# Ternary weights inside the first causal attention, and wider query loads in grouped attention

## The chip, the core and the metric

The kernel is one program on one core of a Trainium2 chip. The metric is the device time of that program in microseconds (us), the median of several runs. The core has a matrix engine (TensorE, PE in the profile, with its weight loads as PEld), VectorE (DVE), ScalarE (ACT), GpSimd (POOL) and a queue engine that starts DMAs (SyncE, SP). Each has its own instruction stream; they meet through semaphores.

## What is computed

Eight layers act in turn on a residual stream X of 2 x 1024 tokens by 256 features. The layers that the change touches are the first three and the fifth:

```python
# 1: causal attention, 16 heads of 128
q, k, v = x @ w_q + b_q, x @ w_k + b_k, x @ w_v + b_v
out = softmax(mask(q k^T / sqrt(128))) v @ w_o + b_o
# 2 and 4: feed-forward layer with ternary weights (2048x256 and 256x1024), groups of 64
w = w_fp32.astype(bfloat16)
scale = clip(mean(abs(w_g)), 1e-8)          # w_g: groups of 64
q = clip(round(w_g / scale), -1, 1)
wq = w + stop_gradient(q * scale - w)
h = silu(x @ wq_gate.T) * (x @ wq_up.T);  y = rms_norm(h) @ wq_proj.T
# 5: grouped-query attention, 32 query heads of 8, 8 key heads, rotary positions, no mask
```

Layer 3 is a delta rule, layers 6 and 8 feed-forward layers with Hadamard-transformed weights, and layer 7 a causal attention with ALiBi. The input of each layer is normalised.

## The kernel before

`program` (line 1784) calls the layers one after another. Each opens a block that all engines enter and leave together. X stays in SBUF for the whole program.

**First attention** (`causal_attention`, line 156, called as "at1"). The work is 32 "halves" n (batch times 16 heads), each of 8 query tiles u, so 256 units U = 8n + u. The order of work is written out by hand: `others(U)` and `turns(U)` list the items that follow the scores of unit U (projections q, k, v; transposed probabilities t; attention times values pv; output projection o; and c, which adds a bias product in every second half). Every item uses one of four PSUM banks in turn, and TensorE waits before item i until VectorE has finished with item i - 4. ScalarE takes the high part of each result (`high`, L521), VectorE the low part (`low`, L616). SyncE loads the weights of a pair of heads (`load`) when GpSimd has split the last pair.

**Ternary stage** (`ternary_weights`, line 667, called as "tq1" and "tq2"). It loads the weights by one DMA for each call and works through 8 and 4 slices of 128 x 512: ScalarE casts a slice to bf16 (L703) and takes its magnitude (L707), TensorE averages it over groups by one matmul (L718), VectorE clips the mean, makes two comparisons and four further steps (L735 to L750), and ScalarE copies the result into the float32r weights (L697).

**Feed-forward layer** (`ffn`, line 753, "ff2" and "ff4"). It begins with statistics on VectorE (L938), an inverse root on GpSimd (L905), the scaled X on VectorE (L950), transposes on TensorE (L835), high part on ScalarE (L886), low part on VectorE (L955), and then the gate and up products (L792), which read the ternary weights.

**Grouped attention** (`grouped_attention`, line 1260). A first block writes the queries and keys, split in three bf16 parts, to DRAM (`qs`, `ks`; L1323). The main block (L1326 on, "ga5m") has 16 units n (batch times key head) in 3 buffer slots, each in two halves of the queries, so 32 halves h. GpSimd issues the loads of a unit in `load` (L1390 for keys, L1395 for queries: 6 + 24 DMAs), three units at the start and then unit n + 2 after the first half of unit n, once TensorE has finished the scores of unit n - 1. For each half, TensorE makes 16 rows of scores (L1455), VectorE takes their maxima (L1538) and copies them, transposed, to mT (L1543); GpSimd splits the maxima in three bf16 parts (`split`, L1404 to L1414), and SyncE copies them into rows 48 to 50 of the query tile by 12 small DMAs (L1435). Only then do the key scores of that half run (L1479), followed by exponentials on ScalarE (L1521) and products with the values (L1492). On GpSimd `split(h + 1)` stands behind the loads that were issued after `split(h)`. On TensorE the first 11 rows of half 1 stand ahead of the first key scores.

Of the kernel before, what the change touches and what calls it, by code (L numbers as in the profile page):

```python
# [155 lines left out]
def causal_attention(nc, name, X, consts, pack, cap_dram, slopes=None, out_bias=None):  # L156
# [9 lines left out]
    with Scope(nc, name) as s:  # L166
# [24 lines left out]
        if out_bias is not None:  # L191
            bsum = s.sb("bsum", [P, D])
            bvT = [s.sb(f"bvT{p}", [P, 2, P], F32R) for p in "hl"]
        S = [s.ps(f"S{i}", [P, SEQ]) for i in range(2)]
# [12 lines left out]
        def others(U):  # L207
# [37 lines left out]
        for x in order:  # L245
            if x[0] not in ("c", "o"):
                high_no[x] = len(high_no) + 1
# [32 lines left out]
        def _(sp):  # L280
# [6 lines left out]

            def load_slope(n):
# [101 lines left out]
        def _(pe):  # L390
# [30 lines left out]
            def use(x):  # L421
# [19 lines left out]
                elif kind == "v":  # L441
# [44 lines left out]
        def _(act):  # L486
# [55 lines left out]

            act.wait_ge(prep_done, 4)
            for what in ("qk0", "v", "qk1", "o") + (("bv",) if out_bias is not None else ()):
                split(0, what)
            for U in range(0, LAST + 1):
                for x in others(U - 1):
                    if x[0] == "o":
                        scaled_out(x)
                    elif x[0] != "c":  # L550
# [6 lines left out]
                m = n // 2 + 1  # L557
                if m < NPAIR:
# [12 lines left out]
        def _(dve):  # L571
# [13 lines left out]
            def low(x):  # L585
                kind, n, i = x
                src = bank(x)[:, :]
                if kind == "c":
# [4 lines left out]
                    return  # L593
                dve.wait_ge(high_done, high_no[x])
# [21 lines left out]
                nc.vector.tensor_tensor(lo, src, hi.bitcast(F32), ALU.subtract).then_inc(low_done, 1)  # L616

# [28 lines left out]
            for U in range(0, LAST + 1):  # L646
# [20 lines left out]
def ternary_weights(nc, name, consts, w_dram, dst, chunks, width):  # L667


    with Scope(nc, name) as s:  # L670
        NCOL = 512
        n = chunks * width // NCOL
        raw = s.sb("raw", [P, chunks * width])
        wb = s.sb("wb", [P, chunks * width], BF16)
        mag = s.sb("mag", [P, 2, NCOL], BF16)
        sc = s.sb("sc", [P, 2, NCOL], BF16)
        up = s.sb("up", [P, NCOL], BF16)
        dn = s.sb("dn", [P, NCOL], BF16)
        sign = s.sb("sign", [P, NCOL], BF16)
        q = s.sb("q", [P, NCOL], BF16)  # L680
        dlt = s.sb("dlt", [P, NCOL], BF16)
        out = [s.sb(f"out{i}", [P, NCOL], BF16) for i in range(2)]
        mean = [s.ps(f"mean{i}", [P, NCOL]) for i in range(2)]
        raw_in, cast_done, mag_done, mean_done, step = (s.sem(x) for x in ("raw", "cast", "mag", "mean", "step"))
        sc_done, out_done, put_done = s.sem("sc"), s.sem("out"), s.sem("put")
        block = s.block()
        dflat = dst.rearrange("p c n -> p (c n)")

        @block.sync
        def _(sp):  # L690
            sp.dma_start(raw[:, :], w_dram).then_inc(raw_in, 16)

        @block.scalar
        def _(act):
            def put(i):
                act.wait_ge(out_done, i + 1)
                nc.scalar.activation(dflat[:, i * NCOL:(i + 1) * NCOL], out[i % 2][:, :],  # L697
                                     ACT.Copy).then_inc(put_done, 1)

            act.wait_ge(raw_in, 16)  # L700
            for i in range(n):
                c = slice(i * NCOL, (i + 1) * NCOL)
                nc.scalar.activation(wb[:, c], raw[:, c], ACT.Copy).then_inc(cast_done, 1)  # L703
# [1256 lines left out]
```

## Time and profile before

| | us |
|---|---|
| median of 3 runs | 3988.59 (3968.72 to 3989.05) |
| the profiled execution, its own time | 3988.94 |
| its span, first to last instruction | 3987.10 |
| first attention | about 10 to 967 |
| ternary stage | 967 to 1031 |
| first ternary feed-forward layer | from 1031 |
| main block of grouped attention | 1749 to 2607 |

Over the span PE is busy 88%, DVE 66%, ACT 56% and POOL 30%. A line of the profile's timeline gives the start, the duration, the engine, the line of the kernel, the tiles written and read, the shapes, how many instructions are merged in it, and in square brackets how long the engine had been idle before and what ended that idle time.

### The profile page before, as it was taken

To read this page: it belongs to the slowest core of one execution; us is meant where nothing else is said; L and a number is where in the kernel's file an instruction comes from. 1 tells how busy PE (TensorE), PEld (TensorE's weight loads), DVE (VectorE), ACT (ScalarE), POOL (GpSimd) and SP (SyncE) were. 2 spreads that over 40 slices of the span, in tenths; PEclk is the share of its full clock that TensorE was granted. 3 is DMA by queue.
4 is the path that set the end of the run, shared out by engine and by line. 5 is a ranking of instruction groups with operands and counts; after the bars stand their busy time and mean duration, and the time that the engine had idled before them with its cause. 6 is when DMAs were issued, how large, how long until landed. Compare 5 with 4: busy or idle time off the path is not lost. (4 is left out here: it accounts for less than half of the span.)

```text
span 3987.1 us, 66189 instructions
## 1 busy us (share of the span) xinstructions
PE 3517.8 (88%) x24420; PEld 2673.4 (67%) x24420; DVE 2631.2 (66%) x4953; ACT 2248.1 (56%) x4552; POOL 1184.8 (30%) x1598
## 2 busy tenths in 40 slices
PE   7999999996578988738888889969799999999979
PEld 6999999996457977512222222248789888888868
DVE  5666666666655665447778777624588788878843
ACT  5777777775433324215667666723467666667732
POOL 2323243331232443253333333030232332232210
PEclk9999999998789998857889888989999999999989
DMA  1000000000000000020000000020111010110010
GB/s 61 17 16 22 22 12 22 22 12 22 11 17 5 0 1 3 18 65 17 22 22 22 22 22 22 2 112 1 43 38 41 29 38 27 42 39 27 27 64 22
DMA packets 46547, 104.76 MB, mean 26 GB/s; under 512 B 28374, under 2 KB 29142, under 8 KB 39976
## 3 DMA queue, kind: packets, MB, share of 16 engines
q1 hardware_dynamic: 18408, 84.83, 6.1%
q0 software_dynamic: 27840, 15.91, 1.7%
q8 instruction: 192, 3.15, 0.3%
q14 instruction: 107, 0.88, 0.1%
HBM read 87.87 MB, written 12.32 MB: 25 GB/s over the span
## 5 line engine op out<-in xcount | busy, mean ns | idle before, releaser
L1538 DVE TENSOR_REDUCE ga5m_nm<-ga5m_M 128x1 f32<-128x1024 f32 x512 | 602.4, 1220 | 171.2 <-PE ga5m_M L1455 161.3
L1521 ACT ACTIVATE ga5m_pr<-ga5m_E 128x512 f32<-128x512 f32 (+1 forms) x683 | 535.0, 811 | 296.3 <-PE ga5m_E L1479 284.9
L352 POOL TENSOR_TENSOR all_X<-all_X,at_part 128x512 f32<-128x512 f32 x256 | 335.4, 1310 | 992.7 <-ACT at_part L532 992.6
L1479 PE MATMUL ga5m_E<-ga5m_Q,ga5m_K 51*128 51x512 bf16 x1024 | 295.4, 419 | 85.6 <-DMA ga5m_Q<-ga5m_mpart 69.7
L417 PE MATMUL at_A<-all_ident,at_prob 128*128 128x128 f32 x2304 | 340.1, 274 | 31.4 <-ACT at_prob L540 22.1
L1492 PE MATMUL ga5m_O<-ga5m_pr,ga_Vx 128*32 128x256 f32 x4096 | 353.2, 424 | 0.0
L1455 PE MATMUL ga5m_M<-ga5m_K,ga5m_Q 48*128 48x512 bf16 x1024 | 255.0, 430 | 61.1 <-DMA ga5m_Q<-ga_qs 43.9
L417 PEld LDWEIGHTS at_A<-all_ident,at_prob 128*128 128x128 f32 x2304 | 265.0, 140 | 60.3 <-DVE at_q1l L600 26.7
L616 DVE TENSOR_TENSOR at_pT1l<-at_A,at_pT1h 128x512 fp32r<-128x512 f32 (+1 forms) x384 | 235.8, 642 | 64.6 <-ACT at_pT1h L521 58.0
L1479 PEld LDWEIGHTS ga5m_E<-ga5m_Q,ga5m_K 51*128 51x128 bf16 x1024 | 68.4, 96 | 313.0 <-issue 164.8
L631 DVE CUSTOM_DVE_ANT_0 at_prob<-at_prob,at_slope 128x128 f32<-128x128 f32 (+7 forms) x256 | 231.5, 904 | 8.8
L965 DVE TENSOR_TENSOR ff_hf<-ff_sil,ff_up 128x512 f32<-128x512 f32 x128 | 87.8, 686 | 220.0 <-ACT ff_sil L871 220.0
L871 ACT ACTIVATE ff_sil<-ff_gate 128x512 f32<-128x512 f32 x128 | 76.8, 600 | 272.1 <-PE ff_up L792 272.1
L631 DVE CUSTOM_DVE_ANT_0 at_S<-at_S,at_cap 128x128 f32<-128x128 f32 (+7 forms) x256 | 194.9, 761 | 44.4 <-PE at_S L395 44.4
L521 ACT ACTIVATE at_pT1h<-at_A 128x512 fp32r<-128x512 f32 (+1 forms) x384 | 202.0, 563 | 28.4 <-PE at_A L417 22.5
L1492 PEld LDWEIGHTS ga5m_O<-ga5m_pr,ga_Vx 128*32 128x32 f32 x4096 | 86.7, 112 | 193.1 <-issue 156.6
L1395 POOL DMA_DIRECT2D ga5m_Q<-ga_qs x384 | 213.7, 583 | 7.6 <-issue 7.6
L625 DVE SCALAR_TENSOR_TENSOR at_prob<-at_S,at_cap 128x128 f32<-128x128 f32 (+7 forms) x256 | 192.5, 752 | 23.5 <-PE at_S L395 23.5
L540 ACT ACTIVATE at_prob<-at_prob,at_nmin 128x128 f32<-128x128 f32 (+7 forms) x256 | 198.0, 773 | 7.6 <-DVE at_nmin L631 7.4
L540 ACT ACTIVATE at_prob<-at_S,at_nmin 128x128 f32<-128x128 f32 (+7 forms) x256 | 189.8, 741 | 1.7 <-DVE at_nmin L631 1.7
L616 DVE TENSOR_TENSOR at_pT0l<-at_A,at_pT0h 128x128 fp32r<-128x128 f32 (+2 forms) x384 | 167.2, 463 | 4.1 <-ACT at_pT0h L521 3.1
L521 ACT ACTIVATE at_pT0h<-at_A 128x128 fp32r<-128x128 f32 (+2 forms) x384 | 147.5, 419 | 28.4 <-PE at_A L417 28.1
(384 smaller groups left out, 10702.1 us busy)
## 6 DMA issues: line engine op xcount, KB each, us to landing
at_raw<-in_pack SPq DMA_DIRECT2D x32, 1027.0 KB, 5.2
at_slope<-in_slopes SPq DMA_DIRECT2D x32, 512.0 KB, 4.2
ga5m_Q<-ga_qs POOLq DMA_DIRECT2D x128, 48.0 KB, 2.2
ga5m_Q<-ga5m_mpart SPq DMA_DIRECT2D x384, 1.0 KB
ga5m_Q<-ga_qs POOLq DMA_DIRECT2D x128, 32.0 KB, 2.2
ga_qs<-ga5s_part SPq DMA_DIRECT2D x6, 512.0 KB
all_X<-in_x SPq DMA_DIRECT2D x1, 2048.0 KB, 7.4
tq_raw<-in_gu SPq DMA_DIRECT2D x1, 2048.0 KB, 7.8
```

What stands on the lines that cost most here:

```text
L352: nc.gpsimd.tensor_tensor(X[:, t:t + 2, :], X[:, t:t + 2, :], part[(i - 1) % 2][:, :, :], ALU.add).then_inc(added, 1)
L417: mm = nc.tensor.transpose(bank(x)[:, (kt % 4) * P:(kt % 4 + 1) * P], prob[u % 4][:, kt * P:(kt + 1) * P], consts["ident"][:, :])
L521: nc.scalar.activation(out, src, ACT.Copy).then_inc(high_done, 1)
L540: nc.scalar.activation(prob[u % 4][:, 0:end], src[:, 0:end], ACT.Exp, bias=nmin[:, at(U):at(U) + 1], scale=-1.0, accum_out=rsum[:, at(U):a ...
L616: nc.vector.tensor_tensor(lo, src, hi.bitcast(F32), ALU.subtract).then_inc(low_done, 1)
L631: nc.vector.tensor_tensor_reduce(out=src, in0=src, in1=add, scale=1.0, scalar=FAR, op0=ALU.add, op1=ALU.min, accum_out=nmin[:, at(U):at(U) ...
L1395: pool.dma_start(Q[n % SLOTS][x][rows, a, :], qs[head:head + 1, q, :, cols].broadcast_to([w, HD, SEQ])).then_inc(q_in[n % SLOTS], 16)
L1455: mm = nc.tensor.matmul(out[:, x * 512:(x + 1) * 512], Q[n % SLOTS][x][at:at + NROW, a, q0:q0 + P], K[n % SLOTS][at:at + NROW, x * 512:(x ...
L1479: mm = nc.tensor.matmul(Eb[:, e % 3, :], K[n % SLOTS][rows, kt * P:(kt + 1) * P], Q[n % SLOTS][0][rows, j // 2, qh * 512:(qh + 1) * 512], ...
L1492: mm = nc.tensor.matmul(Ob[32 * j:32 * j + 32, cols], Vx[:, b * QT + kt, kv, :], pr[:, (k * NQ + j) % NR, cols], start=(kt == 0 and half = ...
L1521: nc.scalar.activation(pr[:, a % NR:a % NR + b - a, :].rearrange("p a n -> p (a n)"), Eb[:, a % 3:a % 3 + b - a, :].rearrange("p a n -> p ...
L1538: nc.vector.tensor_reduce(nm[h % 2][:, r:r + 1], src[:, :], AX.X, ALU.max, negate=True).then_inc(m_read, 1)
```

## The change

The ternary stage goes. `causal_attention` gets an argument `ternary` and makes one slice in each of the halves 0 to 11, kept as bf16; `ffn` converts the twelve slices to float32r at its start, nine on ScalarE and three on GpSimd. In grouped attention, the queries of one unit lie in DRAM so that one DMA brings all four heads (the host permutes the weights' columns to match), each slot holds one query tile where it held two, and six DMAs carry the maxima where twelve did.

```diff
 def others(U):  # first attention
+            if ternary is not None and u == 7 and n < NTERN:
+                out.append(("w", n, 0))
 # SyncE
             for m in range(1, NPAIR):
                 load(m)
+                load_ternary(2 * m - 2)
+                load_ternary(2 * m - 1)      # each 128x512 f32, waits for the cast of the slice before
 # TensorE
+                elif kind == "w":
+                    pe.wait_ge(tmag_done, n + 1)
+                    mm = nc.tensor.matmul(out[:, :], consts["group"][:, :], tmag[:, :], start=True, stop=True)
 # ScalarE
+                if ternary is not None and u == 5 and n < NTERN:
+                    magnitude(n)             # cast to bf16, then Abs
 # VectorE
+                if kind == "w":
+                    dve.wait_ge(full, pos[x] + 1)
+                    nc.vector.tensor_scalar(tsc[:, :], src[:, :], 1e-8, None, ALU.max).then_inc(low_done, 1)
+                    return
...
+                if ternary is not None and 1 <= n <= NTERN and u < 4:
+                    ternary_step(n - 1, u)   # step 0: two comparisons; 1, 2, 3: one tensor_tensor each
+                    if u == 3:
+                        ternary_step(n - 1, 4)
 # ffn, TensorE, behind the transposes and ahead of the gate products
+            if convert is not None:
+                pe.wait_ge(act_conv, len(convert) - POOL_PART)
+                pe.wait_ge(pool_conv, POOL_PART)
 # ffn, ScalarE, ahead of x_high(0, 0)
+            if convert is not None:
+                for dst, src in convert[POOL_PART:]:
+                    nc.scalar.activation(dst, src, ACT.Copy).then_inc(act_conv, 1)
 # ffn, GpSimd, behind inverse_std(0)
+            if convert is not None:
+                for dst, src in convert[:POOL_PART]:
+                    nc.gpsimd.tensor_copy(dst, src).then_inc(pool_conv, 1)
 # grouped attention, stores
-                            dst = qs[m * 16:(m + 1) * 16, k] if i < 2 else ks[:, k]
-                            sp.dma_start(dst, part[i][0:M, k, :]).then_inc(stored, 16)
+                            if i == 2:
+                                sp.dma_start(ks[k], part[i][0:M, k, :]).then_inc(stored, 16)
+                                continue
+                            for t in range(TOK // 512):
+                                sp.dma_start(qs[k, 4 * m:4 * m + 4, :, t], part[i][:, k, t * 512:(t + 1) * 512]
+                                             ).then_inc(stored, 16)
 # grouped attention, loads
-                            for x in range(2):
-                                for a in range(HPG):
-                                    head = kv * NQ + 2 * a + (g + x) % 2
-                                    pool.dma_start(Q[n % SLOTS][x][rows, a, :],
-                                                   qs[head:head + 1, q, :, cols].broadcast_to([w, HD, SEQ])
-                                                   ).then_inc(q_in[n % SLOTS], 16)
+                            pool.dma_start(Q[n % SLOTS][rows, :, :, :],
+                                           qs[q:q + 1, kv, :, 2 * b:2 * b + 2].rearrange("o d t s n -> o d (t s n)")
+                                           .broadcast_to([w, HD, 2 * NQ * 512])).then_inc(q_in[n % SLOTS], 16)
 # grouped attention, maxima
-                            for a in range(HPG):
-                                at = 8 * g + 4 * a
-                                sp.dma_start(Q[n % SLOTS][0][row:row + 1, a, qh * 512:(qh + 1) * 512]
-                                             .rearrange("o (t n) -> o t n", n=P),
-                                             mpart[at:at + 4, x, :]).then_inc(max_in, 16)
+                            sp.dma_start(Q[n % SLOTS][row:row + 1, qh, 2 * g:2 * g + 2, :]
+                                         .rearrange("o s (t n) -> o (s t) n", n=P),
+                                         mpart[8 * g:8 * g + 8, x, :]).then_inc(max_in, 16)
 # program
-            ternary_weights(nc, "tq1", consts, io["gu0"], w1[0], DC, 2 * FF)
-            ternary_weights(nc, "tq2", consts, io["pr0"], w2[0], FC, D)
```

## Rows read from the trace of the kernel before

**Rows 1.** Windows view, busy us (count) by engine, then PE clock, DMA share, GB/s

```profile
967.18:1031.06 63.88, 7.31 (x12) 1.26 (x12) 43.32 (x85) 21.55 (x36) 0.00 (x0) 0.50 0.14 50
50.00:437.00 387.00, 387.00 (x2755) 360.17 (x2754) 248.82 (x573) 276.35 (x646) 117.25 (x110) 1.00 0.06 20
```

**Rows 2.** Timeline at the two ends of the ternary stage

```profile
967.18 0.33 SPq L691 DMA_DIRECT2D tq_raw<-in_gu  x1
...
1031.06 1.40 DVE L938 BATCH_NORM_STATS2 ff_stats<-all_X 128x6 f32<-128x256 f32 x4 [0.97 <-PEq L55]
```

**Rows 3.** Groups by line in the ternary stage: busy us, mean ns of one

```profile
L738 DVE SCALAR_TENSOR_TENSOR tq_up<-tq_sc,tq_wb 128x512 bf16<-128x512 bf16 x12 | 8.3, 693 | 0.4
...
L697 ACT ACTIVATE tern_w<-tq_out 128x512 fp32r<-128x512 bf16 x12 | 7.5, 629 | 28.8 <-DVE tq_out L750 28.8
...
L718 PE MATMUL tq_mean<-tq_mag,all_group 128*128 128x512 bf16 x12 | 7.3, 609 | 53.1 <-ACT tq_mag L707 53.1
```

**Rows 4.** Timeline of VectorE in the first attention: unit 7 of three successive halves

```profile
121.82 1.23 DVE L631 CUSTOM_DVE_ANT_0 at_S<-at_S,at_cap 128x1024 f32<-128x1024 f32 x1 [0.59 <-PE at_S L395]
...
150.48 1.23 DVE L631 CUSTOM_DVE_ANT_0 at_S<-at_S,at_cap 128x1024 f32<-128x1024 f32 x1 [0.60 <-PE at_S L395]
...
179.81 1.23 DVE L631 CUSTOM_DVE_ANT_0 at_S<-at_S,at_cap 128x1024 f32<-128x1024 f32 x1 [0.59 <-PE at_S L395]
```

**Rows 5.** Timeline at the start of half 4 of the first attention

```profile
185.05 1.16 DVE L616 TENSOR_TENSOR at_pT1l<-at_A,at_pT1h 128x512 fp32r<-128x512 f32 x2 [1.58 <-ACT at_pT1h L521]
```

**Rows 6.** Start of the feed-forward layer: timeline, and one GpSimd group

```profile
1033.28 1.04 POOL L905 TENSOR_TENSOR ff_rstd<-ff_vare,all_minus_half 128x4 f32<-128x4 f32 x1
...
1036.94 0.60 ACT L886 ACTIVATE ff_XT0h<-ff_xp 128x512 fp32r<-128x512 f32 x1 [6.19 <-PE ff_xp L835]
...
1039.17 0.79 PE L792 MATMUL ff_gate<-ff_XT0h,tern_w 128*128 128x512 f32 x1 [1.41 <-DVE ff_XT0l L955]
...
L915 POOL COPY ff_acc<-ff_sq 128x512 f32<-128x512 f32 x1 | 0.7, 698 | 13.2 <-ACT ff_sq L882 13.2
```

**Rows 7.** Timeline of the start of grouped attention's main block

```profile
1750.07 3.38 POOL L1381 DMA_DIRECT2D ga5m_K<-in_krows  x6 [38.59 <-POOLq L55]
...
1771.31 1.04 PE L1455 MATMUL ga5m_M<-ga5m_K,ga5m_Q 48*128 48x512 bf16 x4 [43.87 <-DMA ga5m_Q<-ga_qs]
...
1791.21 0.27 DVE L1543 COPY ga5m_mT<-ga5m_M 16x128 f32<-16x128 f32 x1
...
1801.20 0.61 PE L1455 MATMUL ga5m_M<-ga5m_K,ga5m_Q 48*128 48x512 bf16 x2 [0.53 <-DVE ga5m_nm L1538]
...
1802.47 7.50 SPq L1435 DMA_DIRECT2D ga5m_Q<-ga5m_mpart  x12
...
1811.04 0.61 PE L1479 MATMUL ga5m_E<-ga5m_Q,ga5m_K 51*128 51x512 bf16 x2 [9.23 <-DMA ga5m_Q<-ga5m_mpart]
```

**Rows 8.** Query-load issues on GpSimd: ns min/median/max, first and last start

```profile
L1395 POOL DMA_DIRECT2D ga5m_Q<-ga_qs x384: 521/594/644, 1754.0 to 2483.9; - x192
```

**Rows 9.** Timeline of halves 2 to 4 of grouped attention

```profile
1842.53 0.28 DVE L1543 COPY ga5m_mT<-ga5m_M 16x128 f32<-16x128 f32 x1
...
1863.38 0.28 DVE L1543 COPY ga5m_mT<-ga5m_M 16x128 f32<-16x128 f32 x1 [0.44 <-PE ga5m_M L1461]
...
1870.94 0.28 POOL L1404 CAST ga5m_mpart<-ga5m_mT 16x128 bf16<-16x128 f32 x1
...
1879.75 0.61 PE L1479 MATMUL ga5m_E<-ga5m_Q,ga5m_K 51*128 51x512 bf16 x2 [4.01 <-DMA ga5m_Q<-ga5m_mpart]
...
1893.66 0.28 DVE L1543 COPY ga5m_mT<-ga5m_M 16x128 f32<-16x128 f32 x1 [2.18 <-PE ga5m_M L1461]
```

**Rows 10.** Last copy of maxima, and windows without and behind a wait

```profile
2570.14 0.28 DVE L1543 COPY ga5m_mT<-ga5m_M 16x128 f32<-16x128 f32 x1 [1.21 <-PE ga5m_M L1461]
...
1843.00:1864.00 21.00, 20.29 (x205) 5.45 (x197) 19.64 (x20) 16.97 (x22) 10.90 (x23) 1.00 0.10 26
...
1876.00:1894.00 18.00, 14.21 (x73) 3.33 (x73) 8.37 (x10) 7.54 (x10) 0.00 (x0) 0.55 0.00 0
```

More of the change, by code:

```diff
@@ L193, in causal_attention @@
             bvT = [s.sb(f"bvT{p}", [P, 2, P], F32R) for p in "hl"]
+        if ternary is not None:
+            t_src, t_out = ternary
+            NTERN = len(t_src)
+            traw = s.sb("traw", [P, 512])
+            twb, tmag, tsc, tup = (s.sb(f"t{x}", [P, 512], BF16) for x in ("wb", "mag", "sc", "up"))
+            tdn = tmag
+            traw_in, tcast_done, tmag_done = s.sem("traw_in"), s.sem("tcast_done"), s.sem("tmag_done")
+            tstep, tern_done = s.sem("tstep"), s.sem("tern_done")
         S = [s.ps(f"S{i}", [P, SEQ]) for i in range(2)]
@@ L664, in _ @@
                         normalise(1, 2 * (u - 3) + 1)
[L667 to L703, printed above, removed]
-                act.wait_ge(cast_done, i + 1)
-                if i >= 2:
-                    act.wait_ge(mean_done, i - 1)
-                nc.scalar.activation(mag[:, i % 2, :], wb[:, c], ACT.Abs).then_inc(mag_done, 1)
-                if i >= 1:
-                    put(i - 1)
-            put(n - 1)
-        @block.tensor
-        def _(pe):
-            for i in range(n):
-                pe.wait_ge(mag_done, i + 1)
-                if i >= 2:
-                    pe.wait_ge(sc_done, i - 1)
-                nc.tensor.matmul(mean[i % 2][:, :], consts["group"][:, :], mag[:, i % 2, :],
-                                 start=True, stop=True).then_inc(mean_done, 1)
-        @block.vector
-        def _(dve):
-            k = [0]
-            def then(op):
-                k[0] += 1
-                op.then_inc(step, 1)
-                dve.wait_ge(step, k[0])
-            for i in range(n):
-                c = slice(i * NCOL, (i + 1) * NCOL)
-                dve.wait_ge(mean_done, i + 1)
-                nc.vector.tensor_scalar(sc[:, i % 2, :], mean[i % 2][:, :], 1e-8, None, ALU.max).then_inc(sc_done, 1)
-                dve.wait_ge(sc_done, i + 1)
-                nc.vector.scalar_tensor_tensor(up[:, :], sc[:, i % 2, :], 257.0 / 512.0, wb[:, c],
-                                               ALU.mult, ALU.is_lt).then_inc(step, 1)
-                nc.vector.scalar_tensor_tensor(dn[:, :], sc[:, i % 2, :], -257.0 / 512.0, wb[:, c],
-                                               ALU.mult, ALU.is_gt).then_inc(step, 1)
-                k[0] += 2
-                dve.wait_ge(step, k[0])
-                then(nc.vector.tensor_tensor(sign[:, :], up[:, :], dn[:, :], ALU.subtract))
-                then(nc.vector.tensor_tensor(q[:, :], sign[:, :], sc[:, i % 2, :], ALU.mult))
-                then(nc.vector.tensor_tensor(dlt[:, :], q[:, :], wb[:, c], ALU.subtract))
-                if i >= 2:
-                    dve.wait_ge(put_done, i - 1)
-                nc.vector.tensor_tensor(out[i % 2][:, :], wb[:, c], dlt[:, :], ALU.add).then_inc(out_done, 1)
@@ L753, in ffn @@
[L753 removed]
+def ffn(nc, name, X, consts, w1, w2, rms, weights_in=None, convert=None):
     H, L = 0, 1
@@ L1916, in rope, with rotary @@
         return np.ascontiguousarray(np.stack([np.cos(ang), np.sin(ang) * sign], axis=1).astype(f32))
-    def rotary(w, width):
+    spread = np.arange(P) // 4 % 8
+    q_order = np.arange(256).reshape(8, 2, 2, 8).transpose(0, 3, 2, 1).ravel()
+    k_order = np.arange(64).reshape(2, 4, 8).transpose(0, 2, 1).ravel()
+    def rotary(w, width, order=slice(None)):
         wt = w.T
-        swapped = wt.reshape(D, -1, 2, width // 2)[:, :, ::-1, :].reshape(D, -1)
+        swapped = wt.reshape(D, -1, 2, width // 2)[:, :, ::-1, :].reshape(D, -1)[:, order]
+        wt = wt[:, order]
         return np.ascontiguousarray(np.stack([chunks(wt), chunks(swapped)], axis=1))
```

79 lines of the change are left out of this document (58 added, 21 removed).

## The prediction

> **What bounds the kernel now.** I read four views in this order: the table of windows stage by stage, the timeline where stages meet, the groups by line inside the ternary stage, and then, in grouped attention, every copy of maxima to mT, because one copy marks one half.
>
> First attention: in 387 us TensorE is busy for all 387.0, at clock 1.00, VectorE 248.8 and ScalarE 276.4 [rows 1]. So TensorE sets the pace, and what is added to it there adds to the time one for one. VectorE has 138 us free, in 13.5 halves of 28.7 to 29.3 us [rows 4], some 10 us in each.
>
> Ternary stage: from the DMA at 967.18 to the first statistics of the next layer at 1031.06, 63.9 us [rows 2], in which TensorE works 7.3 us and VectorE 43.3 [rows 1]. Nothing else runs beside it.
>
> Grouped attention: mT(2), mT(3) and mT(4) come at 1842.53, 1863.38 and 1893.66 [rows 9]: one half took 20.85 us, the next 30.28. In the short one VectorE is busy 19.6 of 21 us at clock 1.00 [rows 10]; it paces that half. In the long one mT(3) is ready at 1863.38, but GpSimd starts to split it at 1870.94, since it was issuing the loads of a later unit, and TensorE stands idle 4.01 us for the maxima [rows 9]. Then, from 1876 to 1894, it runs only 73 matmuls in 14.2 busy us (195 ns each, against 99 ns before the wait), at a mean granted clock of 0.55, so mostly at the lower level, 1.2 GHz [rows 10]. The timeline has 13 such long halves, one for each unit loaded inside the loop.
>
> **The change part by part.** The sum is made against the profiled execution: span 3987.10, own time 3988.94, which is 0.35 above the median of 3988.59.
>
> *Ternary stage removed: -63.9* [rows 2]. One block boundary stays, as there was one at each end.
>
> *Slices inside the first attention: +7.* TensorE gets 12 matmuls of 512 columns. Halves with the bias item c last 29.33, those without 28.66 [rows 4]; c is six products of 256 columns, so 1536 columns cost 0.67 us and 512 cost 0.22, together 2.7. The upper end for one is its 0.61 in the ternary stage, at half clock [rows 3], together 7.3. VectorE gets 43.3/12 = 3.6 us a slice and ScalarE two activations of some 0.62 [rows 1, 3]; both have that much free in a half. But VectorE's share is bunched at units 0 to 3: the clip and two comparisons of 0.69 each [rows 3] stand at unit 0. The clip falls into the 1.58 us that VectorE waits for ScalarE there [rows 5]; the comparisons come behind it, and push back the low parts that TensorE needs before it may reuse a bank four items later. I put what then reaches TensorE at 0.35 us a slice, 4.2 in all; with 2.7 that is 7. Ends: nothing of it (+3 in all), or all of VectorE's and ScalarE's work, 12 x (3.6 + 1.2) = 58. I am near the low end, because both engines wait, on average, a third of the time. Below +3 it can't go, TensorE having no gap to fill. The SyncE queue gains twelve loads: each waits for the cast of the slice before (unit 5 of a half), and behind it stands the load of a pair's weights, which is released at unit 3 of a later half anyway; no delay.
>
> *Conversion to float32r in the feed-forward layer: 0.* ScalarE is idle until 1036.94, 5.9 us after the layer's start; nine copies of 0.63 [rows 3] take 5.7. GpSimd is free at 1034.3, and TensorE starts the products at 1039.17 [rows 6]: three copies may take 1.6 us each, and the nearest row has 0.70 [rows 6]. What hides them is the chain of statistics, inverse root and transposes. Were that cover gone, it would be 5.7.
>
> *Start of the grouped loop: -18.* Before: 6 + 30 issues, then the first rows at 1771.31, 21.2 us after 1750.07 [rows 7]. That is 0.55 us an issue and 1.4 for landing (one instruction is 0.52 to 0.64 [rows 8]; they overlap a little). Now: 6 + 12 issues, 9.9 + 1.4 = 11.3; I add 1.2, since each query DMA brings four times the bytes: +12.5. mT(0) follows 19.9 later, at +32.4; the 42 issues are over at +23, so the split doesn't wait. What is late next is TensorE's own order: 11 rows of half 1 stand ahead of the first key scores and end 10.6 after mT(0) (1801.81 less 1791.21 [rows 7]), at +43.0. The maxima are there sooner: 12 DMAs took 7.5 us [rows 7], six take 3.75, with 0.3 ahead and 1.1 behind 5.2, at +37.9. First key scores were at +61.0 (1811.04), so 18.0 is gained.
>
> *The 13 waits inside the loop: -123.* From mT(2) to mT(31) are 29 halves in 2570.14 - 1842.53 = 727.6 us [rows 9, 10]. Twelve issues in place of 30 free GpSimd 18 x 0.55 = 9.9 us sooner, at 1861.0, ahead of mT(3). Maxima then land at about 1863.4 + 0.3 + 5.2 = 1868.9, and TensorE wanted them at 1875.7: 6.8 us to spare. With the wait goes the low clock behind it, and VectorE's 20.85 is left: 29 x 20.85 = 604.7, a gain of 122.9. That a half keeps this pace with loads beside it is what the half from 1842.53 shows. Six query issues could each be 1.5 us longer ((6.8 + 2.4)/6) before the wait comes back.
>
> *Stores: +1.* 24 query stores in place of 6, on SyncE, between casts of ScalarE; only the last four can stick out. Bounds 0 and 18 x 0.6 = 11.
>
> Sum: 3988.9 - 63.9 + 7 + 0 - 18 - 122.9 + 1 = **3792 us**.
>
> Two rules beside it. By the Trainium skill's page "DMA: Bandwidth & Descriptors" (section "Why a DMA increments its semaphore by 16 and not by 1"), a DMA uses as many engines as divide the slowest dimension of both sides; a query load repeats three or two times there, so two or three engines would carry 64 KB each. At the page's 436 GB/s over 16 engines I estimate 2.4 us in place of 0.6 for this, and a sum of 3793. No row shows it. Of VectorE and GpSimd the result is a rival below.
>
> **The rivals.**
> (a) *Query issues cost by their bytes.* If GpSimd needs four times 0.58 for four times the bytes, a load takes 6 x 0.55 + 6 x 2.3 = 17 us as before (16.5). The start gains nothing (+18), and of the 4.01 us wait 3.75 are saved by the shorter train of maxima and 0.6 come back: a wait near 1 us. If the clock stays up, that is 13 more: 3823. If it falls as now, a long half is still 27 and the loop loses 13 x 6.4 = 83: 3893. For it: nothing in the trace has 8 KB rows. Against it: the 8, 16 and 24 rows of a load all cost 0.52 to 0.64 [rows 8].
> (b) *The low clock isn't the wait's doing*, and only the waits go: 13 x 4.4 = 57 in place of 123, so 3858. Against it: in every short half the clock is 1.00 although VectorE sets its pace.
> (c) *VectorE and GpSimd get in each other's way in the first attention.* The ternary steps read two SBUF tiles each, and GpSimd adds and splits there. If two of the six are held up by one GpSimd operation of at least 0.70 [rows 6], a slice costs 1.4 more, 17 in all: 3809. The Trainium skill's page "SBUF — State Buffer" (section "Who interferes with whom") says that such an instruction and a GpSimd one that reads SBUF exclude each other for their whole length. The trace before has no such pair that I could time.
> (d) *The other side: the bunched steps cost the first attention its clock.* One wait of some 4 us was enough in grouped attention to halve the speed behind it. If in each of 12 halves TensorE ran at half speed throughout, that is 12 x 28.7 = 344: 4136, slower by 147. It decides from 197/12 = 16.4 us a half on. For it: the first attention has no slack on TensorE. Against it: VectorE has 10 us free in each half, and one burst is 1.4 us.
>
> **How the numbers follow.** The forecast gets 0.72, with its own range 3778 to 3810 (the first attention at +3 to +20, the start and the stores off by 5 either way). (a) 0.08, (b) 0.05, (c) 0.12, (d) 0.03. The range of 8 in 10 takes in (c) and the near end of (a): 3772 to 3830; the low end allows for the spread of 20 us between runs before. A difference of 0.5%, 20 us, is what a measurement tells from none: faster 0.96 (all but (d), less 0.01 kept for no difference), same 0.01, slower 0.03.
>
> **What would show it.** No group of its own between the first attention and the feed-forward layer; halves 1 to 12 of the first attention longer by 0.5 to 0.6 us and the later ones as before; the first gate product some 8.1 us after the statistics begin; first key scores 43 us after the first GpSimd DMA; all copies to mT from the third on 20.8 to 21 us apart, no wait of TensorE for maxima, and clock 1.00 from there to the end of the loop. It would be wrong if halves of 27 us or more are left, if a query issue takes over 2 us, or if halves 1 to 12 grow by more than 2 us.

## The result, and the profile after

The changed kernel takes 3808.23 us, median of 4 runs (3803.93 to 3818.94); the kernel before took 3988.59 on the same chip, median of 3 fast runs (a fourth, in the slow state, took 5820.84 and is left out; with it the median is 3988.82). The ratio is 0.956, with a 95% interval of 0.953 to 0.960. The forecast was 3792 in a range of 3772 to 3830. The profiled execution of the changed kernel is the longest of its four, 3818.94, with a span of 3817.10.

Stage by stage, between the same instructions in the two traces (us). The feed-forward stretches end where the next block loads its rotary table, so the norm behind the layer is in them, and the second one begins with the delta rule's output projection:

| stretch | before | after | forecast of the difference | found |
|---|---|---|---|---|
| first attention and ternary stage | 1031.06 | 974.30 | -56.9 | -56.8 |
| first ternary feed-forward layer and norm | 136.2 | 139.2 | 0 | +3.0 |
| delta-rule block | 240.4 | 250.2 | 0 | +9.8 |
| output projection, second ternary feed-forward layer and norm | 153.5 | 155.8 | 0 | +2.3 |
| store block and first loads, to the first rows | 43.3 | 38.9 | -7.8 | -4.4 |
| first rows to the end of the grouped loop | 832.3 | 702.6 | -132.1 | -129.7 |
| everything else | | | 0 | +6 |

**First attention.** The windows view gives busy us and count by engine, then the granted clock, DMA share and GB/s; below it is the timeline of VectorE at unit 7 of three successive halves, as in [rows 1, 4].

```profile
50.00:437.00 387.00, 386.98 (x2726) 356.55 (x2725) 296.66 (x646) 282.93 (x661) 120.23 (x109) 1.00 0.08 25
```

```profile
123.34 1.23 DVE L686 CUSTOM_DVE_ANT_0 at_S<-at_S,at_cap 128x1024 f32<-128x1024 f32 x1 [0.60 <-PE at_S L414]
...
152.46 1.23 DVE L686 CUSTOM_DVE_ANT_0 at_S<-at_S,at_cap 128x1024 f32<-128x1024 f32 x1 [0.60 <-PE at_S L414]
...
182.46 1.23 DVE L686 CUSTOM_DVE_ANT_0 at_S<-at_S,at_cap 128x1024 f32<-128x1024 f32 x1 [0.60 <-PE at_S L414]
```

VectorE is busy 48 us more in the same 387, TensorE is still never idle, and the clock stays at 1.00. Halves take 29.12 and 30.00 in place of 28.66 and 29.33; the halves from 16 on, which have neither slice nor bias item, take 28.61 in both traces, but for the last two (27.25 and 21.57 in both).

**Feed-forward layer.** The timeline of its start, which answers to [rows 6]:

```profile
974.28 4.78 ACT L869 ACTIVATE tern_w<-tern_q 128x512 fp32r<-128x512 bf16 x9 [1.67 <-PEq L55]
...
977.79 1.84 POOL L910 CAST tern_w<-tern_q 128x512 fp32r<-128x512 bf16 x3
977.86 2.23 DVE L935 TENSOR_SCALAR ff_xn<-all_X,ff_mv,ff_rstd 128x256 f32<-128x256 f32 x4 [1.74 <-POOL ff_rstd L887]
...
983.62 0.77 PE L768 MATMUL ff_gate<-ff_XT0h,tern_w 128*128 128x512 f32 x1 [1.50 <-DVE ff_XT0l L940]
```

The first gate product is 9.3 us behind the first statistics (974.30), where it was 8.1. Four normalise instructions took 2.23 us beside GpSimd's three conversions, 1.38 in the kernel before. This is 1.2 of the +3.0 in the table. The rest differs from run to run: kernels with the same instructions up to there (experiments 3, 4, 5, 8 and 9) take 136.4 to 139.2 for this stretch and 153.1 to 155.8 for the second one.

**Start of the grouped block**, the timeline that answers to [rows 7]:

```profile
1711.68 3.40 POOL L1370 DMA_DIRECT2D ga5m_K<-in_krows  x6 [39.71 <-POOLq L55]
...
1727.58 1.04 PE L1438 MATMUL ga5m_M<-ga5m_K,ga5m_Q 48*128 48x512 bf16 x4 [39.49 <-DMA ga5m_Q<-ga_qs]
...
1747.47 0.27 DVE L1526 COPY ga5m_mT<-ga5m_M 16x128 f32<-16x128 f32 x1
...
1748.12 4.22 SPq L1419 DMA_DIRECT2D ga5m_Q<-ga5m_mpart  x6
...
1757.86 0.64 PE L1462 MATMUL ga5m_E<-ga5m_Q,ga5m_K 51*128 51x512 bf16 x2
```

First rows at +15.9 (forecast +12.5, before +21.2) and first key scores at +46.2 (forecast +43.0, before +61.0). The issues went as forecast and ended at 1721.8; the first rows followed 5.8 us later, the last load having taken 6.2 us from the start of its issue to its landing. What the page and the line's own view say of the query loads, to be held against [rows 8] (ns min/median/max of one issue; then us from issue to landing):

```profile
L1381 POOL DMA_DIRECT2D ga5m_Q<-ga_qs x96: 540/584/627, 1715.7 to 2311.0; - x96
...
DMA to landing us min/median/max: 2.2/3.5/6.3
```

An issue of 64 to 192 KB costs GpSimd what one of a quarter of that cost. Rival (a) is out.

**The loop**, copies of maxima to mT (halves 2, 3, 4 and 31) and the windows that answer to [rows 9, 10]:

```profile
1790.90 0.28 DVE L1526 COPY ga5m_mT<-ga5m_M 16x128 f32<-16x128 f32 x1
...
1811.76 0.28 DVE L1526 COPY ga5m_mT<-ga5m_M 16x128 f32<-16x128 f32 x1 [0.44 <-PE ga5m_M L1444]
...
1833.07 0.28 DVE L1526 COPY ga5m_mT<-ga5m_M 16x128 f32<-16x128 f32 x1 [0.76 <-PE ga5m_M L1444]
...
2396.77 0.28 DVE L1526 COPY ga5m_mT<-ga5m_M 16x128 f32<-16x128 f32 x1 [1.21 <-PE ga5m_M L1444]
```

```profile
1812.00:1833.00 21.00, 19.96 (x200) 5.55 (x198) 19.25 (x19) 16.89 (x24) 1.68 (x5) 1.00 0.03 8
1833.00:1854.00 21.00, 20.30 (x203) 5.95 (x206) 19.76 (x20) 17.42 (x23) 8.48 (x18) 1.00 0.19 46
```

The 29 halves take 605.9 us (forecast 604.7, before 727.6). Of the 121.7 us that went, 60.5 were waiting, as the waits view of the kernel before has it from mT(2) to mT(31) (us in total, times, longest), and the other 61.2 came with the low clock behind the waits:

```profile
PE ga5m_E L1479 <- DMA ga5m_Q<-ga5m_mpart: 60.5, 13, 6.2
```

In the changed kernel the lengths 20.55, 20.86 and 21.32 repeat to the end. Half 3, which took 30.28, takes 21.31. No wait of TensorE for maxima is left, and the clock stays at 1.00.

### The profile page after: what moved, and what is told of

Read it like the earlier page. It is cut to its first block and busy times, and to the rows that moved or that the text cites. A ratio compares the mean times of both kernels' runs of the same rounds, so it can differ in the third digit from the quotient of the medians.

```text
span 3817.1 us, 65706 instructions
## 1 busy us (share of the span) xinstructions
PE 3467.6 (91%) x24420; PEld 2681.7 (70%) x24420; DVE 2637.3 (69%) x4953; ACT 2239.9 (59%) x4549; POOL 1038.3 (27%) x1313
## 5 line engine op out<-in xcount | busy, mean ns | idle before, releaser
L1475 PE MATMUL ga5m_O<-ga5m_pr,ga_Vx 128*32 128x256 f32 x4096 | 324.1, 393 | 0.0
L1462 PE MATMUL ga5m_E<-ga5m_Q,ga5m_K 51*128 51x512 bf16 x1024 | 270.6, 388 | 20.6 <-ACT ga5m_pr L1504 20.1
L1438 PE MATMUL ga5m_M<-ga5m_K,ga5m_Q 48*128 48x512 bf16 x1024 | 232.8, 398 | 59.4 <-DMA ga5m_Q<-ga_qs 39.5
L1633 POOL TENSOR_TENSOR dr3m_WB<-dr3m_W,dr3m_AB 128x128 f32<-128x128 f32 x256 | 108.8, 457 | 166.6 <-DVE dr3m_AB L1690 83.9
```

The costliest lines, as they stand in the source:

```text
L1438: mm = nc.tensor.matmul(out[:, x * 512:(x + 1) * 512], Q[n % SLOTS][at:at + NROW, qh, slot, q0:q0 + P], K[n % SLOTS][at:at + NROW, x * 512 ...
L1462: mm = nc.tensor.matmul(Eb[:, e % 3, :], K[n % SLOTS][rows, kt * P:(kt + 1) * P], Q[n % SLOTS][rows, qh, j % 2 * 2 + j // 2, :], start=Tru ...
L1475: mm = nc.tensor.matmul(Ob[32 * j:32 * j + 32, cols], Vx[:, b * QT + kt, kv, :], pr[:, (k * NQ + j) % NR, cols], start=(kt == 0 and half = ...
```

## The experiments

### 1 and 2. Each half of the change alone

Only the ternary hunks (`causal_attention`, `ffn`, the calls), then only the hunks of `grouped_attention` and its weights' order.

> The ternary half of the change alone: slices made in the first attention, kept as bf16, converted in the feed-forward layer; the grouped-query part is as before. Theory A (the two halves of the change don't touch each other): -63.9 for the stage, +7.1 for the first attention, +1.2 for the later first gate product and up to +3 more in that layer, so -54 to -56 against before, 3933 to 3936 us. Theory B (the few us by which the changed kernel is slower than forecast come from the ternary half, in stages far behind it): the gain is under 50, over 3939 us.

> The grouped-query half alone: stores, loads and maxima DMAs; ternary stage as before. Theory A: -14.8 at the start of the loop, -121.7 between mT(2) and mT(31), +0.9 for the stores, so -136 against before, 3853 us; and no wait for maxima. Theory B (the rest of the miss, some 8 us in other stages, belongs to this half): -125 to -130, 3859 to 3864.

Measured on one chip, where the kernel before took 3986.11: 3937.91 (3935.20 to 3941.10) and 3855.58 (3854.76 to 3856.14), so -48.2 and -130.5, together -178.7. Both together gave -180.4 on their chip. The parts add up. The grouped part came out within 3 us of its theory A (3853), the ternary part 2 us behind the upper end of its own (3936). With the ternary part alone the loop takes 727.5 us from mT(2) to mT(31), with the grouped part alone 605.9. In the trace of the ternary part the first ternary feed-forward layer takes 139.2 again, and layer 7, which no edit touches, 1006.3 in place of 1002.4.

### 3, 4 and 5. What removed the waits: fewer loads, or fewer maxima DMAs

Experiment 3 issues the maxima as before, experiment 4 the loads, experiment 5 both; the new layout in DRAM and SBUF stays in all three. The cuts are shortened.

```diff
-    sp.dma_start(Q[n % SLOTS][row:row + 1, qh, 2 * g:2 * g + 2, :], mpart[8 * g:8 * g + 8, x, :])
+    for a in range(2):                                            # 3 and 5: 12 a half
+        sp.dma_start(Q[n % SLOTS][row:row + 1, qh, 2 * g + a, :], mpart[8 * g + 4 * a:..., x, :])
...
-    pool.dma_start(Q[n % SLOTS][rows, :, :, :], qs[q:q + 1, kv, :, 2 * b:2 * b + 2])
+    for t in range(2):                                            # 4 and 5: 30 a unit
+        for v in range(2):
+            pool.dma_start(Q[n % SLOTS][rows, t, 2 * v:2 * v + 2, :], qs[q:q + 1, kv, :, 2 * b + t, 2 * v:2 * v + 2])
```

> The changed kernel with 12 DMAs of maxima a half in place of 6, one for each slot; loads as in the change. Theory A (the loads hold the split up, the train of maxima doesn't matter): the train takes 7.5 us in place of 4.2 and still ends 1.5 us or more before TensorE wants it, at the start too (8.9 against 10.6 us); time as the changed kernel, within 3 us. Theory B (merging the maxima is part of what removed the waits): waits of TensorE for maxima come back, up to 3.3 us in a half, and with the low clock behind them up to +85.

> The changed kernel with each query load cut in four, so 30 issues a unit as before, layout and maxima as in the change. Theory A (the count of GpSimd issues decides): the first rows come 18 x 0.6 = 11 us later, and in the long halves the split starts some 7.6 us after mT again; with the short train of maxima they land 12.8 us after mT and TensorE wants them at 12.3, so a wait of 0.5 to 1 us in 13 halves. If so short a wait leaves the clock at 1.00: +11 +13 x 0.7 = +20 against the changed kernel. Theory B (any wait brings the low clock): 13 x 6 more, +95. Theory C (the old layout, not the count, made the loads slow): +11 at the start and nothing in the loop.

> The changed kernel's layout, but with the old counts of both: 30 GpSimd issues a unit and 12 DMAs of maxima a half. Each count alone cost 0 (maxima) and 34 us (issues) between mT(2) and mT(31). Theory A (one deadline: split late plus train of maxima against the time at which TensorE wants the maxima, and the low clock past some length of wait): the gaps of 1.2, 3.2 and 1.1 us become 4.4, 6.4 and 4.3 as in the kernel before, the stretch takes 727 us again, and the time is 3930 to 3940. Theory B (the new layout also helps by itself): the stretch stays below 715.

Times: 3804.90 (3800.89 to 3811.45), 3853.67 (3847.84 to 3863.95), 3941.59 (3940.44 to 3943.67), so theory A for experiment 3, and for experiment 5 theory A with a time 1.6 us above its range. From mT(2) to mT(31), in us:

| | 6 maxima DMAs a half | 12 maxima DMAs a half |
|---|---|---|
| 12 issues a unit | 605.9 | 605.9 |
| 30 issues a unit | 640.2 | 732.2 (kernel before: 727.6) |

The two counts meet in one deadline. Where it waits, TensorE wants the maxima of a half 11.8 to 12.4 us after mT. They are there at: start of the split, plus 0.3, plus the train of DMAs (4.0 us for 6, 7.4 for 12), plus 1.1 for its landing. With the split at once both trains are early; the 12 DMAs end their issues 8.0 us after mT. With the split 7.1 to 9.5 us late, TensorE waits 0.8 to 3.1 us for the short train and 4.1 to 6.4 for the long one. Experiment 4, timeline of half 5 and of half 7, and a window behind the wait of each (busy by engine, then clock):

```profile
1865.83 0.28 DVE L1528 COPY ga5m_mT<-ga5m_M 16x128 f32<-16x128 f32 x1
...
1875.25 0.28 POOL L1392 CAST ga5m_mpart<-ga5m_mT 16x128 bf16<-16x128 f32 x1
...
1880.69 0.60 PE L1464 MATMUL ga5m_E<-ga5m_Q,ga5m_K 51*128 51x512 bf16 x1 [3.07 <-DMA ga5m_Q<-ga5m_mpart]
...
1917.03 0.28 DVE L1528 COPY ga5m_mT<-ga5m_M 16x128 f32<-16x128 f32 x1 [0.76 <-PE ga5m_M L1446]
...
1924.19 0.28 POOL L1392 CAST ga5m_mpart<-ga5m_mT 16x128 bf16<-16x128 f32 x1
...
1929.93 0.37 PE L1464 MATMUL ga5m_E<-ga5m_Q,ga5m_K 51*128 51x512 bf16 x1 [0.99 <-DMA ga5m_Q<-ga5m_mpart]
```

```profile
1931.00:1938.00 7.00, 6.30 (x64) 1.99 (x56) 6.61 (x8) 5.87 (x8) 0.00 (x0) 1.00 0.00 0
1881.00:1895.00 14.00, 14.00 (x77) 3.31 (x76) 7.87 (x8) 7.75 (x10) 0.00 (x0) 0.50 0.00 0
```

Behind the wait of 0.99 us the clock stays at 1.00 (2.4 GHz). Behind the one of 3.07 it is at 0.50 (1.2 GHz) through the window. Nine of the 13 waits are of the first kind (0.8 to 1.1 us) and four of the second (2.8 to 3.1); behind the three of 2.80 the low level lasted some 6 us, behind the one of 3.07 some 15. The waits views of experiments 4 and 5, over the same 13 halves (us in total, times, longest):

```profile
PE ga5m_E L1464 <- DMA ga5m_Q<-ga5m_mpart: 19.1, 13, 3.1
```

```profile
PE ga5m_E L1466 <- DMA ga5m_Q<-ga5m_mpart: 62.3, 13, 6.4
```

In experiment 4 the loop is 34.3 us longer than in the changed kernel: 19.1 of waiting, and 15.2 that go with the low clock behind four of the waits. In experiment 5 it is 126.3 longer: 62.3 and 64.0. The second number of each pair is the difference, not a measurement of its own. Experiment 4 fell between its theories (+45 against the changed kernel's median, +49 against experiment 3, forecast +20 or +95). The start cost the 11 us of theory A (mT(2) is 10.9 later from the first store on, 113.2 in place of 102.3), half of it by late rows and half by a late first split, but four waits were three times as long as expected, because the split is late by 9.1 to 9.4 us in every third unit and not by 7.6. The layout gives nothing by itself: experiment 5 is within 5 us of the kernel before in the loop, on the long side.

### 6. The slices without VectorE's bunched steps

```diff
-    (steps 0 to 3: two comparisons, subtract, multiply, subtract)
+    only the last add, at step 4, behind the clip
```

The clip, the slice's matmul and ScalarE's two activations stay; what is left out is the rounding, so the weights are no longer ternary.

> The changed kernel without VectorE's steps 0 to 3 of a ternary slice (two comparisons, subtract, multiply, subtract): clip, matmul, ScalarE's two activations and one last add stay; the weights of the second layer are then not ternary. Theory A (of the 0.45 and 0.67 us that halves 1 to 12 grew, 0.22 is the matmul and the rest the bunched VectorE steps): halves at 28.9 and 29.55, first attention 3 to 4 us shorter than in the changed kernel. Theory B (the rest comes from ScalarE's activations at unit 5 or the clip ahead of the slice's matmul): halves stay at 29.1 and 30.0.

Measured: 3805.17 (3798.47 to 3813.80). Unit 7 of three successive halves comes at 121.47, 150.59 and 180.38, so halves of 29.12 and 29.79: the short ones are as before this edit, the long ones 0.2 shorter. From unit 7 of half 0 to unit 7 of half 12 that is 353.6 in place of 354.7, and 347.9 in the kernel before. Theory B holds in the main: the bunched steps cost 1.1 us in all. Where the rest goes is in the changed kernel's timeline, at the slice's matmul in half 3 (TensorE, then VectorE):

```profile
154.30 0.39 PE L473 MATMUL at_A<-at_tmag,all_group 128*128 128x512 bf16 x1
...
155.51 0.95 PE L436 MATMUL at_A<-all_ident,at_prob 128*128 128x128 f32 x7
156.47 0.38 PE L412 MATMUL at_A<-at_wo0h,at_bvTh 128*128 128x256 f32 x1
```

```profile
155.12 0.69 DVE L652 TENSOR_TENSOR at_V0l<-at_A,at_V0h 128x512 fp32r<-128x512 f32 x1 [0.50 <-ACT at_V0h L543]
155.73 0.68 DVE L628 TENSOR_SCALAR at_tsc<-at_A 128x512 bf16<-128x512 f32 x1
```

The item at 156.47 takes the bank that the slice's average was in, and VectorE's clip reads that bank until 156.41. The view of the clip's tile says for how long its reader was waited for (us, times), and says the same in experiment 6:

```profile
PEld at_A L412: 2.9, 12
```

So the +7.1 is 1.1 for the bunched steps, which experiment 6 shows, 2.9 for the clip and the rest, some 3, for the twelve matmuls: matmuls around one of them stand 0.22 further apart than their like. The last two are read from the trace; no run takes away the clip or the matmul alone.

### 7. All conversions on ScalarE

```diff
-            POOL_PART = 3
+            POOL_PART = 0
```

> The changed kernel with all 12 conversions on ScalarE, none on GpSimd. Theory A (VectorE's four normalise instructions took 2.23 in place of 1.38 us because GpSimd's conversions ran beside them): normalise takes 1.38 again; ScalarE is done at +6.4 and TensorE starts the products some 8.6 us after the first statistics, 0.7 sooner than with three on GpSimd; total within 1 us. Theory B (normalise is slow because of ScalarE's conversions): 2.2 us stays and the start is later than 9.3.

```profile
978.21 1.38 DVE L935 TENSOR_SCALAR ff_xn<-all_X,ff_mv,ff_rstd 128x256 f32<-128x256 f32 x4 [1.74 <-POOL ff_rstd L887]
```

Theory A: normalise takes 1.38 again, and the first gate product comes 8.47 behind the statistics in place of 9.32. The time, 3815.81 (3800.05 to 3822.45), can't show 0.85 us. The other 0.36 against the kernel before (8.11) stays: in both traces GpSimd's first instruction begins 0.73 us behind the first aggregate of the statistics, where it was 0.46. No run shows why.

### 8 to 12. The start of the grouped block

Experiment 8 moves the first unit's loads; 9 changes only the order of rows in a load (of the keys' loads too, which the cut leaves out); 10 is 8, 9 and 7 together; 11 is the changed kernel again, beside 9 and 10; 12 adds a hold to 10.

```diff
+    load(sp, 0, (0,), q0_in[0])                  # 8, 10, 12: at the head of SyncE's stream
+    load(act, 0, (1,), q0_in[1])                 # 8, 10, 12: at the head of ScalarE's
...
-    pe.wait_ge(ones_in, 16 * 2 * SLOTS)          # 8, 10, 12: now ahead of the first key scores
...
-    qs[q:q + 1, kv, :, 2 * b:2 * b + 2].rearrange("o d t s n -> o d (t s n)").broadcast_to([w, HD, 4096])
+    qs[q:q + 1, kv, :, 2 * b:2 * b + 2].rearrange("o d t s n -> d o (t s n)").broadcast_to([HD, w, 4096])  # 9, 10, 12
...
+    pool.wait_ge(q0_in[0], 16 * 6); pool.wait_ge(q0_in[1], 16 * 6)      # 12: ahead of load(1)
```

> The changed kernel with the first unit's 12 loads on SyncE's and ScalarE's queues, six each, at the head of the block; GpSimd issues the rows of ones and units 1 and 2 beside them; TensorE waits for the rows of ones at the first key scores and not at its start. Theory A (the first rows wait for 6 + 12 issues one after the other): first rows at 6 x 0.6 + 2 to 3.5 of landing = +6 to +7 in place of +15.9, and all behind it 9 us sooner: 3799. Theory B (landing of the big loads, 5.8 us behind the last issue, is what the first rows wait for, because 24 later loads share the DMA engines): they land no sooner than +11, and the gain is under 5 us.

> The changed kernel with the rows of a load in another order: the eight dimensions outermost and the one to three repeats inside (the sum over rows is the same), issues and bytes as in the change. In the changed kernel query loads of 24, 16 and 8 rows of 8 KB land 3.3, 3.3 and 4.4 us after their issue, about 8 x 0.5 us for each, as if three, two and one DMA engines carried them. Theory A (the outermost dimension of a load sets how many engines carry it, and that is the late landing at the start): all of them land in about 2 us, and the first rows come 3 to 4 us sooner, +12 to +13 in place of +15.9 after the first GpSimd DMA; first key scores as much sooner; the loop stays at 605.9; total 3 to 4 us less, 3804. Theory B (the late landing is the traffic of units 1 and 2, whatever the order): landing stays at 3.3 to 4.4 and the first rows at +15.9.

> Three edits on the changed kernel: rows of the loads spread as in the kernel above, the first unit's loads on SyncE's and ScalarE's queues with the rows of ones waited for at the first key scores only, and all conversions on ScalarE. With only the second, the first rows came 8 us later than in the changed kernel, since the packets of the two hardware queues were on the wire until 20 us after the last of them was issued. Theory A (few engines for each load): now the first rows are at +7 to +9 after the first issue of the block, 7 to 9 us sooner than in the changed kernel, and the gate product 0.85 us sooner: 8 to 10 us less, 3799. Theory B (traffic of the later units, or the hardware queues themselves): first rows later than +13, no gain.

> The changed kernel again, on the same chip as the two above, as their base. What the two of its traces have in common is the kernel's; what differs is the execution's. Theory A (the 10.6 us more in the delta-rule block and the 3.0 and 2.3 in the two feed-forward layers belong to the execution, since a kernel with the same instructions up to there had 240.6 in place of 250.2): runs spread over 10 to 20 us between about 3800 and 3820, and this trace shows 240 or 250 in the delta-rule block. Theory B (they belong to the change): 250, 139.2 and 155.8 again in every trace.

> The kernel with all three edits (spread rows, first unit on SyncE's and ScalarE's queues, conversions on ScalarE), and GpSimd issues the loads of units 1 and 2 only after the first unit's have landed. Without the hold the first unit's last packets ended 10.7 us after the block's first issue and the first rows came at +12.5. Theory A (GpSimd's 24 loads took the DMA engines from the first unit): packets end at +7 to +8, first rows at +8 to +9, and as the first split at +28 still finds GpSimd free (24 x 0.58 = 14 us behind +8), all of it reaches the end: 3.5 to 4.5 less, about 3797. Theory B (the first unit's own packets, 96 of 8 KB at 0.5 us and their order, set the pace): first rows at +12 to +12.5, no gain.

Experiment 8 ran on one chip, 9, 10 and 11 on a second, 12 on a third. All columns in us; the last two count from the first cast of the store block.

| | median us (range) | first rows after the block's first DMA | to first rows | to mT(31) |
|---|---|---|---|---|
| changed kernel | 3808.23 (3803.93 to 3818.94) | 15.9 | 38.9 | 708.1 |
| 11, the same | 3805.63 (3803.13 to 3821.96) | 16.3 | 39.3 | 708.4 |
| 8 | 3810.75 (3806.21 to 3812.16) | 24.7 | 47.0 | 715.9 |
| 9 | 3805.11 (3802.86 to 3817.09) | 14.1 | 37.1 | 705.9 |
| 10 | 3801.42 (3793.39 to 3808.42) | 12.5 | 34.8 | 703.0 |
| 12 | 3808.93 (3807.18 to 3810.74) | 9.8 | 32.1 | 701.4 |

Experiment 8 came out worse than either of its theories, and taught most. Its issues were over at 1701.4, 4.7 us after the first, and the first rows still came at 1721.44. First DMA and first rows in 8, then in 10:

```profile
1696.71 0.86 SPq L1375 DMA_DIRECT2D ga5m_K<-ga_ks  x1
...
1721.44 1.04 PE L1445 MATMUL ga5m_M<-ga5m_K,ga5m_Q 48*128 48x512 bf16 x4 [47.57 <-DMA ga5m_Q<-ga_qs]
```

```profile
1696.20 0.79 SPq L1375 DMA_DIRECT2D ga5m_K<-ga_ks  x1
...
1708.68 1.04 PE L1445 MATMUL ga5m_M<-ga5m_K,ga5m_Q 48*128 48x512 bf16 x4 [35.64 <-DMA ga5m_Q<-ga_qs]
```

Same bytes, same queues, same issues; in this block only the order of the rows inside the loads differs (GpSimd's too), and the last load of the two hardware queues landed 13 us sooner. The trace has 48 packets of 8 KB on each of these queues, 0.45 and 0.52 us each. In 8 they end 16.3 and 19.3 us after the start of the last issue, in 10 5.6 and 6.5. The packets of 8 KB of experiment 8 start in threes 0.3 us apart for the loads that repeat three times and, on the queue that ended first, in pairs for the one that repeats twice, as if three and two DMA engines carried 8 packets each; the eight packets of a load without repeats start within 0.4 us on either queue, as on eight engines and not on one, which the expectation of experiment 9 took from the landing on GpSimd's queue. An engine that takes part in all six query loads would then carry 8 packets of each of four and one of each of two: 34 x 0.5 = 17 us. Its 34 packets of 2 KB of the six key loads, at 0.10 and 0.16 us each, make that about 21, an estimate; from the first packet to the last it was 22.

By the Trainium skill's page "DMA: Bandwidth & Descriptors" (section "Why a DMA increments its semaphore by 16 and not by 1"), a DMA runs on the largest number of engines, at most 16, that divides the slowest dimension (dimensions of size 1 left aside) of both sides, on a hardware queue the lowest-numbered ones, and on GpSimd's queue consecutive ones that move on from DMA to DMA. The traces don't name the engines, but agree with both halves: with two or three repeats outermost the hardware queues piled up (last packet 16.3 and 19.3 us after the last issue in 8, 5.6 and 6.5 in 10), while on GpSimd's queue the order of the rows moved the first rows by 1.8 to 2.2 us only (experiment 9, between its theories). GpSimd's own loads suffered beside the pile: one of them took 16.0 us from issue to landing in 8, and none over 6.7 in 10.

Experiment 12 shows the other part: with GpSimd's 24 loads held back, the first rows come 2.7 us sooner still, at +9.8. The line is experiment 12's first rows; its first DMA is at 1707.37:

```profile
1717.19 1.04 PE L1447 MATMUL ga5m_M<-ga5m_K,ga5m_Q 48*128 48x512 bf16 x4 [32.96 <-DMA ga5m_Q<-ga_qs]
```

Its first key scores are at +40.1 and no split is late. That is a little behind its theory A (+8 to +9), and of the 2.7 us only 1.6 are left at mT(31). Both causes of the late landing are real; the second is shown with the first unit on the hardware queues only.

Experiment 10 lies between its theories (+7 to +9, or later than +13) with +12.5. In their traces 10 and 12 are 5 and 7 us ahead of the changed kernel up to mT(31), and 0.85 in the feed-forward layer. That can't be called shown in whole times: 10 has 3801.42 against 3805.63 with overlapping runs, and 12 ran on another chip, where the delta-rule block took 250.0.

**Delta-rule block.** No edit touches it. The windows view over this block in the changed kernel, then in experiment 8, whose instructions up to there are the same:

```profile
1180.90:1431.10 250.20, 241.18 (x1536) 222.04 (x1537) 159.14 (x388) 82.25 (x272) 108.85 (x256) 0.95 0.00 1
```

```profile
1178.70:1419.30 240.60, 231.65 (x1536) 212.31 (x1537) 159.20 (x388) 82.24 (x272) 108.05 (x256) 0.99 0.00 1
```

The 10 us are TensorE at the lower clock level: in the changed kernel's trace from 1407 to the end of the block (1431), in experiment 8 only behind it. The block has 240.4 to 240.6 in the kernel before, experiments 5, 8, 9, 10 and 2, 239.2 in 1, and 250.0 to 250.6 in both traces of the changed kernel and in 3, 4, 6, 7 and 12. Theory A of experiment 11 is half shown: its profiled run is 16 us longer than the other three, and kernels with equal instructions up to there have either value; but the changed kernel itself showed 250 in both of its traces, and 139 and 155.8 in the two feed-forward stretches.

## Why the prediction was right

- *Ternary stage, -63.9*: right. From unit 7 of the last half to the first statistics it is 14.96 us in place of 78.81, so 63.9 less; the next layer starts 56.8 us sooner, the 7.1 between going to the slices.
- *Slices, +7*: the sum was right, its second term by the wrong cause, and that 0.24 + 0.09 comes so near the 0.35 is luck. The matmuls cost about 0.22 each as taken. The 0.35 a slice put on "the comparisons come behind it, and push back the low parts" is 0.09. The clip, said to fall "into the 1.58 us that VectorE waits", costs 0.24: it does find VectorE free, but it releases its bank 0.25 us after TensorE wants it. What binds TensorE there is when a bank comes free, not how busy VectorE is.
- *Rival (c)*, VectorE and GpSimd holding each other up, is a true mechanism at almost the size given, and costs nearly nothing. A multiply of a slice in half 2, and its like in half 3 beside GpSimd's addition to X:

```profile
135.17 0.43 DVE L667 TENSOR_TENSOR at_tmag<-at_tup,at_tsc 128x512 bf16<-128x512 bf16 x1
...
164.77 1.29 POOL L371 TENSOR_TENSOR all_X<-all_X,at_part 128x512 f32<-128x512 f32 x1
...
165.00 1.35 DVE L667 TENSOR_TENSOR at_tmag<-at_tup,at_tsc 128x512 bf16<-128x512 bf16 x1
```

The second ends 0.28 us behind GpSimd's instruction. Two of six steps of a slice are held up so, 1.4 to 1.7 us in all, where 1.4 was forecast. VectorE has the room: without the steps only 1.1 us in twelve slices came back. The Trainium skill's page "SBUF — State Buffer" (section "Who interferes with whom") has it that a VectorE instruction with two inputs in SBUF and a GpSimd one that reads SBUF exclude each other for their whole length. Here the trace agrees: the multiply took 1.35 us in place of 0.43.
- *Conversions, 0*: wrong by 1.2, of which experiment 7 takes away 0.85. Of what the products wait for, the forecast looked at when conversions end (979.6, 4.0 us ahead of the products), not at what they do to the statistics' chain beside them.
- *Start, -18*: -14.8. The step that failed is the landing: 1.4 + 1.2 us were taken, and it was 5.8. Experiments 8 to 12 split it in few DMA engines for each load (1.8 to 2.2 us of it on GpSimd's queue, experiment 9) and the 24 loads behind. The Trainium skill's rule was in the prediction, at an estimated 2.4 us for a load; that such loads meet on the same engines, with each other and with those of the next units, was not.
- *Waits, -123*: -121.7. The mechanism is shown: deadline, lateness and clock, each by experiments 3 to 5. VectorE's pace is 20.89 on average, not 20.85. The waits come to 60.5, or 4.65 each, where the sum for rival (b) took 4.4; with 4.65 that rival gives 3854 in place of 3858.
- *Stores, +1*: +1.0 in the store block.
- *Rival (b)* is out: bringing back waits of 19.1 us brought back 15.2 more with the low clock, behind the four longest alone (experiment 4), and waits of 62.3 brought 64.0 (experiment 5). *Rival (d)* is out by the clock of 1.00 in the first attention.

The forecast missed by 16 us, or 27 for the profiled run. About 7 of these are the change's own: 3.3 at the first rows, 2.4 in the loop, 1.2 in the feed-forward layer. The rest lies in stages whose instructions did not change, above all in the delta-rule block. What sets its clock in one execution and not in another stays open.

## What to carry to other kernels

Where an engine waits at a deadline, write down all the terms that must fit ahead of it before removing one: here fewer issues took away all 122 us with either train of maxima, while the shorter train alone took 87 and left 34. A short wait (here up to 1.1 us) cost itself; the longer ones (2.8 to 6.4 us) cost about as much again in clock. When several small DMAs are merged into large ones, as here, the issue stays cheap and the landing need not: put a dimension outermost that many DMA engines can share, before moving such loads to a hardware queue.

## What the runs showed of the hardware

- A GpSimd issue took 540 to 627 ns whether it moved 64 or 192 KB, as it did for a quarter of that.
- In the grouped loop waits of TensorE of 0.8 to 1.1 us left the granted clock at 1.00; those of 2.8 to 3.1 us (experiment 4) and of 4.1 to 6.4 (experiment 5) were followed by 0.50.
- Two or three repeats outermost in a load's shape: on SyncE's and ScalarE's queues the last of 48 packets of 8 KB each ended 16.3 and 19.3 us after the last issue (experiment 8). With the eight dimensions outermost: 5.6 and 6.5 (experiment 10).
- The delta-rule block took 240.6 us at a mean granted clock of 0.99 (experiment 8) and 250.2 at 0.95 (changed kernel), with the same instructions up to there.
- Normalising four tiles took 1.38 us alone and 2.23 beside GpSimd's conversions; a bf16 product of two tiles 0.43 alone and up to 1.36.
